# A routing stage whose norm root moves into the round of its statistics, and whose second slot table moves into the expert stage

## The reference, cut to what matters

```python
def _L1_gnn_ref(x, adj, weight, bias):
    d_inv_sqrt = (jnp.sum(adj, axis=-1) + 1e-05) ** (-0.5)
    adj_norm = d_inv_sqrt[..., :, None] * adj * d_inv_sqrt[..., None, :]
    support = jnp.einsum('bni,io->bno', x, weight)
    return jnp.einsum('bnm,bmo->bno', adj_norm, support) + bias
def _L1_ffn_ref(x, router_w, w1, w2, w3):
    logits = flat @ router_w.T
    topk_probs, topk_idx = jax.lax.top_k(jax.nn.softmax(logits, axis=-1), 2)
    topk_probs = topk_probs / (jnp.sum(topk_probs, axis=-1, keepdims=True) + 1e-09)
    h = _silu(einsum('nc,ehc->neh', flat, w1)) * einsum('nc,ehc->neh', flat, w3)
    return einsum('ne,nec->nc', gates, einsum('neh,ech->nec', h, w2))
x = x + _L1_gnn_ref(_layernorm(x), adj, ...)
x = x + _L1_ffn_ref(_layernorm(x), ...)
```

## Time and profile before

| | us |
|---|---|
| median of 3 runs | 1110.66 (1109.28 to 1110.87) |
| the profiled execution, and its span | 1106.77, 1104.9 |
| busy in the span: PE, DVE, ACT, POOL | 986.0, 788.8, 691.8, 504.4 |
| routing stage, from the first instruction to the last scatter's end | 654.19 to 786.96 |
| expert stage, from its first instruction to the end | 789.80 to 1104.9 |

### The profile page before, as it was taken

How to read it: one execution, slowest core, us unless ns; L and a number is a source line. 1 busy time by engine, 2 the same in 40 slices (tenths; PEclk the granted TensorE clock), 3 DMA queues, 4 the chain that set the end, 5 groups by cost and what they waited for, 6 DMA issues and landing times. The chain is left out here.

```text
span 1104.9 us, 23153 instructions
## 1 busy us (share of the span) xinstructions
PE 986.0 (89%) x6744; PEld 869.1 (79%) x6744; DVE 788.8 (71%) x2044; ACT 691.8 (63%) x1467; POOL 504.4 (46%) x479
## 2 busy tenths in 40 slices
PE   4999999999999579999999968783299999799997
PEld 4988988988998446777777757673299999799997
DVE  5788888888887668899999846998455555355553
ACT  5576566656656369889888828882155555355553
POOL 5233233223322016767776536567434444344454
PEclk9999999999999798999999979985599999899999
DMA  5311221131110023342322219734245443333331
GB/s 178 97 48 49 69 74 47 47 95 47 47 38 1 25 81 77 77 77 77 64 68 64 38 52 314 212 131 145 85 129 151 122 125 111 89 96 99 93 100 48
DMA packets 82408, 99.09 MB, mean 90 GB/s; under 512 B 9243, under 2 KB 68258, under 8 KB 82186
## 3 DMA queue, kind: packets, MB, share of 16 engines
q1 hardware_dynamic: 72122, 74.24, 24.8%
q0 software_dynamic: 8752, 21.25, 5.5%
q10 hardware_dynamic: 1440, 2.43, 0.6%
HBM read 72.26 MB, written 27.02 MB: 90 GB/s over the span
## 5 line engine op out<-in xcount | busy, mean ns | idle before, releaser
L1754 PE MATMUL e_p_y<-w,e_gT 128*128 (+1 forms) x852 | 118.3, 275 | 0.0
L1701 DVE TENSOR_TENSOR e_g<-e_sl,e_p_h 128x342 f32<-128x342 f32 x142 | 72.6, 511 | 63.7 <-ACT e_sl L1679 57.8
L1665 POOL DMA_INDIRECT sorted_scratch<-e_xg x71 | 69.0, 972 | 91.5 <-DVE e_xg L1711 88.4
L1683 ACT ACTIVATE e_gT<-e_p_gx 128x384 f32<-128x384 f32 x142 | 69.6, 490 | 63.8 <-PE e_p_gx L1744 63.8
L1679 ACT ACTIVATE e_sl<-e_p_h 128x342 f32<-128x342 f32 x142 | 64.9, 457 | 70.0 <-PE e_p_h L89 69.8
L1663 POOL DMA_INDIRECT out<-e_xg x71 | 68.9, 970 | 86.2 <-DVE e_xg L1711 78.8
L1754 PEld LDWEIGHTS e_p_y<-w,e_gT 128*128 128x128 f32 (+1 forms) x852 | 106.1, 191 | 0.5 <-issue 0.4
L87 PE MATMUL e_p_h<-w_hi,e_xT_hi 128*128 x284 | 104.4, 368 | 1.7 <-issue 0.9
L1705 DVE TENSOR_TENSOR e_xT_lo<-e_p_gx,e_xT_hi 128x128 fp32r<-128x128 f32 x142 | 41.4, 291 | 86.4 <-ACT e_xT_hi L1687 86.1
L967 DVE SCALAR_TENSOR_TENSOR m_c<-m_p_x,m_vecs,m_c 128x506 f32<-128x506 f32 (+2 forms) x144 | 95.4, 734 | 4.8 <-ACT m_c L850 4.8
L89 PE MATMUL e_p_h<-w_hi,e_xT_lo 128*128 x284 | 92.0, 324 | 0.0
(11 more groups left out here) (377 smaller groups left out, 3314.8 us busy)
## 6 DMA issues: line engine op xcount, KB each, us to landing
e_xg<-sorted_scratch SPq DMA_DIRECT2D x142, 130.0 KB, 2.1
m_cum<-cum_scratch SPq DMA_DIRECT2D x16, 1024.0 KB, 7.9
g_adjT<-in_adjT SPq DMA_DIRECT2D x16, 512.0 KB, 3.8
g_adj<-in_adj SPq DMA_DIRECT2D x16, 512.0 KB, 5.0
c_adjT<-in_adjT SPq DMA_DIRECT2D x16, 512.0 KB, 6.8
x_tokens<-in_x SPq DMA_DIRECT2D x16, 256.0 KB, 4.8
sorted_scratch<-nothing SPq DMA_DIRECT2D x2, 1040.0 KB, 10.0
sorted_scratch<-nothing SPq DMA_DIRECT2D x12, 130.0 KB, 3.4
```

The lines of the kernel that those rows point to most:

```text
L1665: sent = pool.indirect_dma_start(sorted_dram[1], home, xg[:, b], None, bounds_check=ROWS - 1, oob_is_err=False)
L1683: act.activation(gT[:, c % D3], p_gx[i % 2][:, 0:len(CH)], ACT.Copy).then_inc(q["gT_ready"], 1)
L1701: dve.tensor_tensor(g[:, i % D3], sl[:, i % 2], p_h3[i % 2][:, 0:HP], ALU.mult).then_inc(q["g_ready"], 1)
L1754: last = pe.matmul(p_y[d % 2][:, 0:P], gT[0:r, d % D3, k], w2k[:, bass.ts(e, P)], start=k == 0, stop=k == len(CH) - 1)
```

## The change

First, `NORM2` becomes `OUT`, so that logarithm, exponential and root of a step stand in the same round as its update, and all later parts stand one round sooner, and the loop is one round shorter. On ScalarE the logarithm and exponential move behind the two copies; on VectorE the root moves to the end of the round. Second, the slot table of the second pass leaves the routing stage: a class `Slots` holds the tiles and makes a table in four pieces. The first pass's table is made where it was, the second's inside VectorE's loop of the expert stage, ahead of ticks 12, 16, 20 and 24. SyncE and TensorE get a wait for it where the second pass starts.

```diff
-    NORM2 = OUT + 1
-    TURN2, COPY2, LOG, TAKE = OUT + 2, OUT + 3, OUT + 3, OUT + 4
+    NORM2 = OUT
+    TURN2, COPY2, LOG, TAKE = OUT + 1, OUT + 2, OUT + 2, OUT + 3
@@ ScalarE, round i
-                if live(c):
-                    act.wait_ge(q["mv2_done"], T * (c + 1))
-                    act.activation(logs[:], mv[:, c % 2, :, 1], ACT.Ln, bias=eps[:, 0:1]).then_inc(q["logs_done"], 1)
-                    act.activation(rough[:], logs[:], ACT.Exp, scale=-0.5).then_inc(q["rough_done"], 1)
                 if live(e):
                     act.activation(xT2[:, e % 2], p_xT2[:], ACT.Copy).then_inc(q["xT2_ready"], 1)
                 if live(f):
                     act.activation(logits[...], p_log[:], ACT.Copy).then_inc(q["log_ready"], 1)
+                if live(c):
+                    act.wait_ge(q["mv2_done"], T * (c + 1))
+                    act.activation(logs[:], mv[:, c % 2, :, 1], ACT.Ln, bias=eps[:, 0:1]).then_inc(q["logs_done"], 1)
+                    act.activation(rough[:], logs[:], ACT.Exp, scale=-0.5).then_inc(q["rough_done"], 1)
                 if live(s):
...
@@ VectorE, round i: the block "if live(c): ... scale, shift" moves from the round's start to its end
...
@@ VectorE, behind the loop
-            for k in range(TOPK):
-                then(dve.tensor_tensor(past[:], ..., per_expert(ends[:, k]), ALU.is_ge))
...
+            for piece in range(Slots.PIECES):
+                slots.piece(dve, 0, piece, source, words, then)
@@ Slots.piece(dve, k, n, ...)
+        if n == 0:
+            then(dve.tensor_tensor(past[:], ..., per_expert(self.ends[:, k]), ALU.is_ge))
+            then(dve.tensor_reduce(exp_f[:], past[:], AX.X, ALU.add))
+        elif n == 1:
+            then(dve.tensor_tensor(part[:], past[:], per_expert(self.tiles[:, k]), ALU.mult))
+            then(dve.tensor_reduce(first[:], part[:], AX.X, ALU.add))
+        elif n == 2:
...
@@ expert_phase
+    TABLE_TICKS = range(XG, XG + 4 * Slots.PIECES, 4)
@@ SyncE
                 if u == 0 and k:
                     sp.wait_ge(q["padded"], 16 * EX)
+                    sp.wait_ge(q["second_table"], 1)
@@ VectorE, tick i
+                if i in TABLE_TICKS:
+                    slots.piece(dve, 1, TABLE_TICKS.index(i), source, words, then)
+                    if i == TABLE_TICKS[-1]:
+                        dve.sem_inc(q["second_table"], 1)
@@ TensorE, expert_of
+                if u == 0 and k:
+                    pe.wait_ge(q["second_table"], 1)
```

More of the change, by code:

```diff
@@ L1215, with __init__, sb, piece @@
 HOME, GATE = (P, P + 2), (P + 1, P + 3)
+class Slots:
+    PIECES = 4
+    def __init__(self, nc, ctx):
+        def sb(name, shape):
+            return ctx.enter_context(nc.sbuf_tensor("slots_" + name, shape, F32))
+        self.slot_no, self.tiles, self.ends = sb("no", [P, PASS]), sb("tiles", [P, TOPK, EX]), sb("ends", [P, TOPK, EX])
+        self.past, self.part = sb("past", [P, PASS, EX]), sb("part", [P, PASS, EX])
+        self.exp_f, self.first = sb("exp_f", [P, PASS]), sb("first", [P, PASS])
+    def piece(self, dve, k, n, source, words, then):
+        past, part, exp_f, first, slot_no = self.past, self.part, self.exp_f, self.first, self.slot_no
+        by_slot = [P, PASS, EX]
+        def per_expert(v):
+            return v.rearrange("p (a e) -> p a e", a=1).broadcast_to(by_slot)
+        if n == 0:
+            then(dve.tensor_tensor(past[:], slot_no[:].rearrange("p (s a) -> p s a", a=1).broadcast_to(by_slot), per_expert(self.ends[:, k]), ALU.is_ge))
+            then(dve.tensor_reduce(exp_f[:], past[:], AX.X, ALU.add))
[3 more added lines that the diff above has]
+        elif n == 2:
+            then(dve.tensor_tensor(first[:], slot_no[:], first[:], ALU.subtract))
+            then(dve.scalar_tensor_tensor(out=first[:], in0=exp_f[:], scalar=float(PASS), in1=first[:], op0=ALU.mult, op1=ALU.add))
+            then(dve.tensor_scalar(source[:, k], first[:], float(P), None, ALU.mult))
+            then(dve.tensor_scalar(exp_f[:], exp_f[:], float(EX - 1), None, ALU.min))
+        else:
+            quad = exp_f[:].rearrange("p (u j) -> p u j", j=QUAD)
+            for j in reversed(range(QUAD - 1)):
+                then(dve.scalar_tensor_tensor(out=quad[:, :, j], in0=quad[:, :, j + 1], scalar=float(EX), in1=quad[:, :, j], op0=ALU.mult, op1=ALU.add))
+            then(dve.tensor_copy(words[:, k], quad[:, :, 0]))
 def expert_weights(nc, ctx):
@@ L1224, in expert_weights, with dispatch_phase @@
     return pair("w1", [P, EX, HP]), pair("w3", [P, EX, HP]), w2
-def dispatch_phase(nc, w, X, norm, dinv, rows, source, words, filled, pad_at, nothing, experts, adjT_dram, sorted_dram, eye):
+def dispatch_phase(nc, w, X, norm, dinv, rows, source, words, filled, pad_at, nothing, slots, experts, adjT_dram, sorted_dram, eye):
     ADJ = 5
     XS, AGG, OUT = 0, 1, 2
-    NORM2 = OUT + 1
-    TURN2, COPY2, LOG, TAKE = OUT + 2, OUT + 3, OUT + 3, OUT + 4
+    NORM2 = OUT
+    TURN2, COPY2, LOG, TAKE = OUT + 1, OUT + 2, OUT + 2, OUT + 3
     GROUP = 2
@@ L1582, in _, with expert_phase @@
                     last.then_inc(q["log_done"], 1)
[L1585 removed]
+def expert_phase(nc, source, words, filled, pad_at, nothing, slots, experts, sorted_dram, out_dram, eye):
     XG, D3 = 12, 3
@@ L1693, in _, with then @@
                 dve.memset(p_gx[k][:], 0.0).then_inc(q["p_g_clear"], 1)
+            count_ = [0]
+            def then(ins):
+                count_[0] += 1
+                ins.then_inc(q["chain"], 1)
+                dve.wait_ge(q["chain"], count_[0])
             for i in range(-TURN, TICKS + DOWN):
                 a, d = i + TURN, i - DOWN
+                if i in TABLE_TICKS:
+                    slots.piece(dve, 1, TABLE_TICKS.index(i), source, words, then)
+                    if i == TABLE_TICKS[-1]:
+                        dve.sem_inc(q["second_table"], 1)
                 if live(i):
@@ L1778, in build @@
         experts = expert_weights(nc, ctx)
+        slots = Slots(nc, ctx)
         sorted_dram = (scratch["sorted0"], scratch["sorted1"])
[L1780 to L1781 removed]
+        dispatch_phase(nc, ins, X, norm, inv[:, 0], rows, source, words, filled, pad_at, nothing, slots, experts, ins["adjT"], sorted_dram, eye)
+        expert_phase(nc, source, words, filled, pad_at, nothing, slots, experts, sorted_dram, out_dram.rearrange("b n d -> (b n) d"), eye)
 def kernel(x, adj, L0_gnn_w_se, L0_gnn_b_se, L0_gnn_conv1_w, L0_gnn_bn1_g, L0_gnn_bn1_b, L0_gnn_bn1_m, L0_gnn_bn1_v,
```

47 lines of the change are left out of this document (14 added, 33 removed).

## The result

The changed kernel takes **1131.3 us** in the median of 4 runs (1127.9 to 1133.8) beside 1110.8 for the kernel before (1109.3 to 1110.9): a ratio of 1.0193, 95% interval 1.0172 to 1.0214. It is 20.6 us slower. The forecast was 1126.3 with a range of 1119.5 to 1134.0: the sign and the range hold, the size is 5 us short. The ratios in this document are estimated over the runs themselves, so they are not quite the quotient of two medians (1131.3 / 1110.8 is 1.0185).

What follows compares the result with a forecast made beforehand. GpSimd's train of 64 scatters ends the routing stage, VectorE pacing it up to group 5. Slower rounds 11.2, ScalarE behind pick rounds 1.0 and TensorE's clock 3.4 sum to +15.6 on 1110.66: 1126.3 us, range 1119.5 to 1134.0.

Steps and rivals of the forecast that it cites:

- The circle: Routing loop: update, statistics, logarithm, xs, aggregate copy, TensorE's product, next update wait in turn; no round shorter than 6.18 us.
- The walk to update 15: Routing rounds from VectorE's update of step 0 to step 15: 94.55 us, plus 1.0 for ScalarE behind five pick rounds.
- TensorE's clock: Routing stage: c_p_out takes 1.97 instead of 1.13 at the low clock in four of 15 rounds, +3.4 us.
- The rival of a slow TensorE: TensorE at 1.2 GHz in most routing rounds: +24.8 us, 1135.5; chance 0.09.
- From update 15 to group 5: From VectorE's update of step 15 to the first GpSimd scatter of group 5: 4.90 us.
- The last 24 scatters: GpSimd's train from group 5 on is saturated and takes 33.64 us, whatever else happens.
- The table: Second slot table moved from VectorE's routing tail (5.11 us) to the expert stage: worth nothing, hidden in both.
- The rival of one round sooner: If the circle did not bind, every scatter group would be ready a round earlier: 5.5 us faster, 1105.2; chance 0.04.

Runs made afterwards that it cites:

- a link lengthened by 0.52: The changed kernel with one more unread ScalarE copy between the exponential and xs in rounds with a live step; 1135.3 us, ratio 1.0216.
- the filling: The changed kernel with unread matmuls in TensorE's waits, in rounds with ranks placed behind the aggregate; 1125.8 us, beside 1129.0 for the changed kernel in that set.
- the root alone: The changed kernel with the second slot table put back behind the first in the routing stage; 1132.3 us, ratio 1.0201 to the kernel before.
- the table alone: The kernel before with only the second slot table moved into the expert stage; 1112.4 us, ratio 1.0017.
- the copy moved sooner: Kernel before with second table moved, root unmoved, ScalarE's copy of the turned step behind the same round's aggregate copy, later parts a round sooner; 1108.8 us, ratio 0.9984.
- the kernel with that circle opened: The changed kernel with ScalarE's logarithm and exponential moved behind xs and the aggregate copy, still in the same round; 1128.2 us, ratio 1.0159.
- the kernel without splits: The changed kernel without VectorE's two subtractions that split the expert weights at the routing stage's end; 1123.3 us, ratio 1.0113.

## Why the prediction came out as it did

- **The circle** (6.18 a round): right, 6.16 at full clock. The logarithm moved by itself gives the whole slowdown, and a link lengthened by 0.52 adds 6.7 over 15 rounds.
- **The walk to update 15** (94.55, and 1.0 behind pick rounds): nearly right. The changed kernel takes 102.96, and 6.4 of it are slow products, so 96.6 at full clock against 95.55 (by the same sum 97.1, 96.6 and 96.3 in the three other traces of these rounds). Rounds at full clock behind a pick round are 6.40 in the trace with the filling, 0.2 above the circle, as taken; the first pick round took 7.98 instead of 7.53, and the weights' copy on ScalarE (768.95, 2.46 long where xs takes 1.63) lengthened the last round, which I had not priced.
- **TensorE's clock** (+3.4, four rounds in fifteen): the term that was mis-sized for the changed kernel. Eight of sixteen products are slow in both of its traces, and together they take 7.3 and 6.9 more than at 1.13. In the two other traces with the same rounds five are slow, for 3.7 and 4.0, so there the term was met, and the traced stage of the root alone is 18.2 longer than before (149.67 - 131.47) and not 21.1: what the rounds cost here lay between 3.7 and 7.3, and I gave it the low end as if it were fixed. I read the rate of falls off one trace of the kernel before, with rounds of 5.19 in the mean (the trace of the table alone, with the old rounds too, has three slow products and not one), and carried it over to rounds of 6.86 (102.96 / 15), in which TensorE idles 24.8 us in place of 13.4. The rival of a slow TensorE, with a chance of 0.09, was half true: slow were up to half of the products, not most.
- **From update 15 to group 5** (4.90): 779.12 - 774.21 = 4.91 (5.76 in the changed kernel's second trace). **The last 24 scatters** (33.64): 34.28; of the 0.6, 0.2 is the long scatter of 2.81 in place of 2.60, the rest are three of 1.01 to 1.27.
- The sum: 21.1 measured less 15.6 forecast is 5.5. Of it 3.0 is the clock behind the first product (6.4 less 3.4), 1.0 the walk, 0.6 the train. The last 0.9 is the first product, which was slow too. It stands ahead of the circle and is slow as well in the traces of the table alone and of the copy moved sooner, so that part is not the change's.
- **The table** (nothing): right on both sides, 1.0017 (0.9996 to 1.0039) by itself; the late gating product of 1.06 was hidden as argued. The cover at the routing stage's end was 6 us in the changed kernel and 0.85 with the table back.
- **The rival of one round sooner** fell. It was not only the logarithm, as I had it: the kernel with that circle opened shows the second one, through the root at the end of VectorE's round and ScalarE's normalising, which no step of the prediction priced. That circle is read from the waits in that trace; no experiment took it away.
- Open: the 4 us of the kernel without splits that its train does not explain (2 by the changed kernel's second median), and what decides how many products are slow in one execution.

## What to carry to other kernels

Taking a round out of a software pipeline is only a gain if no circle of one round is closed by it: add up producer, consumer and everything that the consumer's engine has queued behind the wait, back to the producer, and compare it with the round that you have. What a longer round does to an engine off the path (here TensorE, which idles more and is granted less clock) belongs into the sum as a rate that grows with the idling, read from more than one execution, and not as the rate of the old kernel. Latency gained ahead of a train need not arrive at its end: here 3.7 us at the first scatter were 2.3 at the last.

## What the runs showed of the hardware

VectorE and GpSimd held each other up where both worked on SBUF. Two scatters of the train took 2.81 and 2.60 instead of 0.97 while VectorE subtracted two SBUF operands, and none did without the subtractions. The other way round a VectorE instruction of 128x4 took 1.19 instead of 0.16 beside GpSimd's bias add, and ended with it (674.10 + 1.19 against 672.78 + 2.48); in the changed kernel two such instructions, at 710.23 and 711.39, took 1.12 and 1.19 beside a bias add that ended at 712.57. The Trainium skill (SBUF — State Buffer, Who interferes with whom) gives the second as an exclusive lock on a shared port, and the trace agrees; for descriptor making it infers that a tensor_tensor does not hold it up, and the scatters of 2.6 and 2.8 were held up by one all the same. Which part of a scatter was held up, the making of its descriptors or the reading of its destinations from SBUF, no run shows.

The granted clock differs between executions of the same rounds. Five or eight of sixteen products ran at the low level in four traces of these rounds, and the first product of the stage was slow in five of the twelve traces, with and without the change.
